# Four transformer layers on one core: the f16 half of the 32-head attentions' probabilities is cast by VectorE instead of computed by a second exponential on ScalarE

## What is computed

```python
q = einsum('bse,ef->bsf', query, Wq)      # 32 heads of 16
k = einsum('bse,ef->bsf', key, Wk)        # 8 heads of 16
v = einsum('bse,ef->bsf', value, Wv)
q, k = q * cos + rotate_half(q) * sin, k * cos + rotate_half(k) * sin   # first layer alone
scores = einsum('bhqd,bhkd->bhqk', q, repeat(k, 4)) / sqrt(16)
out = einsum('bhqk,bhkd->bhqd', softmax(scores), repeat(v, 4))
return einsum('bsf,fe->bse', out, Wo)
```

## Time and profile before

| | |
|---|---|
| median of three runs | 2558.53 us |
| lowest, highest | 2553.02, 2559.68 us |
| the profiled execution | 2555.08 us |
| its span, first to last instruction | 2553.1 us |
| granted TensorE clock, mean share of full speed | 0.918 |
| busy: TensorE, VectorE, ScalarE, GpSimd | 2287.4, 1725.6, 1254.1, 189.3 us |

### The profile page before, as it was taken

How to read it: one execution, slowest core, us unless ns; L and a number is a source line. 1 busy time by engine, 2 the same in 40 slices (tenths; PEclk the granted TensorE clock), 3 DMA queues, 4 the chain that set the end, 5 groups by cost and what they waited for, 6 DMA issues and landing times.

```text
span 2553.1 us, 41949 instructions
## 1 busy us (share of the span) xinstructions
PE 2287.4 (90%) x15456; PEld 1292.8 (51%) x15456; DVE 1725.6 (68%) x4380; ACT 1254.1 (49%) x3499; POOL 189.3 (7%) x191
## 2 busy tenths in 40 slices
PE   4778799989999999999985888799889999999978
PEld 2333344445666666666653444344455555555544
DVE  6443455576777777777767453565778888888873
ACT  3333421136656665666552453433366666666631
POOL 1333300000000000000000133200000000000010
PEclk8666799999999999999998686699989999999999
DMA  4000011110010010010000000001111101110000
GB/s 168 17 9 1 1 50 50 58 59 26 17 42 26 18 42 27 18 42 10 26 17 17 1 34 1 17 17 50 66 42 43 42 18 43 42 42 20 34 1 33
DMA packets 10297, 82.37 MB, mean 32 GB/s; under 512 B 1376, under 2 KB 1376, under 8 KB 2528
## 3 DMA queue, kind: packets, MB, share of 16 engines
q1 hardware_dynamic: 10080, 79.54, 8.6%
HBM read 77.44 MB, written 2.10 MB: 31 GB/s over the span
## 4 chain that ended last, share of the span: by engine, by line
PE 48%; DVE 25%; issue 13%; ACT 10%; POOL 3%; DMA 0%; DVEq 0%; POOLq 0%; ACTq 0%; SPq 0%
PE bank L463 40%; ACT probs L1171 4%; DVE probs L1669 3%; ACT pT_hi L1238 3%; DVE rawmax L1637 3%; DVE qT_lo L1714 2%; DVE pT_lo L1730 2%; POOL pT_lo L419 2%; POOL qT_lo L419 1%; PE bank L810 1%; PE bank L793 1%; DVE oT_lo L1683 1%; PE bank L563 1%; DVE wa_lo L1327 1%; DVE masked L1645 1%
## 5 line engine op out<-in xcount | busy, mean ns | idle before, releaser
L463 PE MATMUL bank<-xnT_hi,wa_hi 128*128 128x512 f16 x736 | 280.6, 381 | 3.2 <-PE bank L463 2.6
L463 PE MATMUL bank<-xnT_lo,wa_hi 128*128 128x512 f16 x736 | 280.1, 381 | 0.0
L463 PE MATMUL bank<-xnT_hi,wa_lo 128*128 128x512 f16 x736 | 280.0, 380 | 0.0
L463 PE MATMUL bank<-wo_hi,oT_hi 128*128 128x512 f16 x576 | 228.0, 396 | 24.7 <-DVE oT_lo L1683 16.2
L463 PE MATMUL bank<-wa_hi,xnT_hi 128*128 128x512 f16 (+3 forms) x672 | 226.8, 343 | 10.0 <-DVE wa_lo L1327 5.2
L1171 ACT ACTIVATE probs<-bank,negmax,rms_r 128x256 f32<-128x256 f32 x256 | 141.0, 560 | 189.2 <-DVE negmax L1642 189.2
L463 PE MATMUL bank<-wo_lo,oT_hi 128*128 128x512 f16 x576 | 228.4, 397 | 0.0
L463 PE MATMUL bank<-wo_hi,oT_lo 128*128 128x512 f16 x576 | 228.3, 396 | 0.0
L463 PE MATMUL bank<-wa_lo,xnT_hi 128*128 128x512 f16 (+3 forms) x672 | 227.1, 343 | 0.0
L463 PE MATMUL bank<-wa_hi,xnT_lo 128*128 128x512 f16 (+3 forms) x672 | 226.7, 343 | 0.0
L1494 DVE TENSOR_REDUCE negmax_n<-bank 128x4 f32<-128x512 f32 x128 | 87.5, 689 | 152.6 <-PE bank L563 152.1
(11 more groups left out here) (256 smaller groups left out, 5555.5 us busy)
## 6 DMA issues: line engine op xcount, KB each, us to landing
raw<-in_w_qkv_dram SPq DMA_DIRECT2D x18, 1536.0 KB, 6.6
raw<-in_w_out_dram SPq DMA_DIRECT2D x18, 1024.0 KB, 4.8
raw<-in_w_ffn_dram SPq DMA_DIRECT2D x15, 1024.0 KB, 4.8
raw<-in_w_ffn0d_dram SPq DMA_DIRECT2D x7, 512.0 KB, 3.4
x<-in_x_dram SPq DMA_DIRECT2D x1, 2048.0 KB, 8.4
expert_b<-in_expert_b_dram SPq DMA_DIRECT2D x1, 2048.0 KB, 9.3
raw<-in_w_ffn3b_dram SPq DMA_DIRECT2D x2, 1024.0 KB, 4.9
out_dram<-x SPq DMA_DIRECT2D x1, 2048.0 KB, 6.3
```

The source lines that it names most:

```text
L463: mm = pe.matmul(dst, l, r, start=start and k == 0, stop=stop and k == n - 1)
```

## The change

ScalarE's second exponential of each unit (L1099) goes, with its wait for `ng_attn`; `ng_exp` is now raised by the first. VectorE gets `probs_hi(j)`: it waits for `ng_exp`, from the fifth unit also for attend(j-4), copies `probs` to the f16 half and raises the new semaphore `ng_phi`, on which GpSimd's `probs_lo(j)` waits in place of `ng_exp`. It stands at the head of step j in VectorE's list. That is so in both stages, 64 units each.

```diff
@@ GpSimd, probs_lo @@
                 J = n * UNITS + j
-                pool.wait_ge(ng_exp, J + 1)
+                pool.wait_ge(ng_phi, J + 1)
@@ ScalarE, soft @@
                     if j >= 4:
                         act.wait_ge(ng_plo, J - 3)
-                        act.wait_ge(ng_attn, J - 3)
                     p32, hi, lo = p_ring(j)
-                    act.activation(p32, bank[PT0 + j % 2][:, :], ACT.Exp)
-                    act.activation(hi, bank[PT0 + j % 2][:, :], ACT.Exp).then_inc(ng_exp, 1)
+                    act.activation(p32, bank[PT0 + j % 2][:, :], ACT.Exp).then_inc(ng_exp, 1)
@@ VectorE, narrow @@
+                def probs_hi(j):
+                    J = n * UNITS + j
+                    dve.wait_ge(ng_exp, J + 1)
+                    if j >= 4:
+                        dve.wait_ge(ng_attn, J - 3)
+                    p32, hi, lo = p_ring(j)
+                    dve.tensor_copy(hi, p32).then_inc(ng_phi, 1)
+
                 q_part(0)
                 kv_part(0)
                 for j in range(-G, UNITS + 5):
                     b, g = divmod(j, G)
                     f, p = b + 1, b + 2
+                    if 0 <= j < UNITS:
+                        probs_hi(j)
                     if g == 0 and f < B:
                         q_rows(f)
```

More of the change, by code:

```diff
@@ L340, in build @@
                              "nb_max_rows", "nb_inv", "nb_on", "nb_olo", "nb_y", "ng_max"))
+        ng_phi = sem("ng_phi")
         n_consts, nb_qn, nb_kn, nb_parts, ng_plo = (sem(n) for n in ("n_consts", "nb_qn", "nb_kn", "nb_parts", "ng_plo"))
```

## The result

| | before | changed |
|---|---|---|
| median of six runs | 2558.5 us | 2572.0 us |
| lowest, highest | 2553.0, 2562.1 | 2565.9, 2579.6 |
| the profiled execution | 2555.08 | 2567.67 |
| its span | 2553.1 | 2565.5 |
| busy ScalarE, VectorE | 1254.1, 1725.6 | 1193.5, 1778.9 |

The ratio is 1.0053, with a 95% interval of 1.0032 to 1.0073: slower by 13.5 us, where 41 were forecast (2596.5, range from 2574). The sign was right and the size was not. The changed kernel's six runs lie in two groups, three at 2566 to 2568 us and three at 2576 to 2580, and its profile is of one of the lower three.

A forecast was written before the change was run, and what follows sets the result against it. TensorE, busy 90%, was taken as the bound, so its waits for VectorE count. 16.4 + 1 + 9.8 - 2.8 + 5 + 12 = 41.4 us on 2555.1 gave 2596.5, range 2574 to 2616.

The forecast's parts named there:

- Prices: 128 exponentials of 0.59 us removed from ScalarE, 128 casts of 0.428 us added on VectorE.
- Step g = 2, +1.17: Both stages, 14 blocks: row maximum 1.45 us later behind the cast, k rows 0.28 earlier; 1.17 each, +16.4 us.
- Steps g = 3 to 5, +1: Maximum again 1.45 us late, but projection matmuls between the two scores cover it; +1 us in all.
- Step g = 6, second stage, +1.4: Seven blocks: cast ahead of max_split adds 0.38 us, its subtraction waiting for GpSimd at the port 1.0; +9.8 in all.
- Step g = 6, first stage, -0.4: Seven blocks: GpSimd's L419 starts earlier, so max_split's subtraction ends at 222.0 instead of 222.39; -2.8 us in all.
- The tails, +5: Units 57 to 63, both stages: the next cast can't run beside L419, 1.68 us per unit; +5 us together.
- The clock, +12: Second stage: more idle at g = 2 and g = 6 lowers the clock, about half of 22.6 us; first stage 0.
- Rival (e): Faster: new idle keeps blocks at clock 0.93, each giving back up to 6.8 us; six give 2543.6; chance 0.06.
- the signs of being right: Listed trace signs of a right forecast, among them second-stage blocks of 30 to 34 us at a clock near 0.66.
- (c): Second stage: VectorE's subtraction gets ahead of GpSimd, 7 us less, and no clock is lost: 2577; chance 0.07.
- (a): Whole kernel: the waits as worked out, but no loss of clock: 2555.1 + 29.4 = 2584.5 us; chance 0.20.
- (d): The late maximum at g = 2 costs nothing, gains and losses within 5 us: about 2557; chance 0.08.

The follow-up runs named there:

- portfree: Changed kernel, with GpSimd's subtraction of the unit at g = 6 held until VectorE's max_split is over: 2560.1 us, ratio 0.9981 to the kernel before.
- tail26: Changed kernel with the casts of g = 2 and g = 6 moved later, and ScalarE's second exponential kept in each stage's last block: 2535.9 us, ratio 0.9905.

## Why the prediction was right or wrong

**Prices**: right. The cast took 0.427 us for 0.428.

**Step g = 2, +1.17**: right as a wait. The row maximum came 1.84 behind its scores (s+1.90 was forecast), the step grew by 1.56 and the one before it shrank by 0.32.

**Steps g = 3 to 5, +1**: right where there are projections: at the full level g = 5 took 2.58 in place of 2.48, the 0.1 that was forecast. But in block b = 6 there is nothing to cover the maxima, and these steps grew by 2.0 in each stage. The prediction had named that price ("each step would cost up to 1.4") and had not seen where it applies.

**Step g = 6, second stage, +1.4**: right. The step g = 6 took 3.45 in place of 2.10, and `portfree` shows the port as the cause of 1.0 of it.

**Step g = 6, first stage, -0.4**: right for six blocks, 4.04 in place of 4.50. The seventh, b = 6, has no rotary products and went from 2.15 to 3.71, as in the second stage. What I had not seen either is that a wait of 1.8 could be taken away at this step.

**The tails, +5**: somewhat too much. In the terms of the earlier trace rows, GpSimd's subtractions alone, seven of them span 1.2 us more in the first stage and 2.6 more in the second:

```profile
281.21:291.59 10.38, 8.07 (x7) 0.69 0.01 2
1634.43:1647.05 12.62, 8.84 (x7) 0.60 0.07 11
```

In the first stage they come every 1.52 us, where 1.68 was forecast. At the turned scores, which run ahead of them, 1.2 and 1.4 had arrived by unit 63. `tail26` gave 3.5 of such time back.

**The clock, +12**: here the prediction failed. It measured about -13 (-16 in the first stage, +2.6 in the second) by the estimate from two blocks and -16 (-18.1 and +1.7) by TensorE's busy time. That is 25 to 28 us below the forecast, and the miss of the whole sum, in the profiled execution, is 41.4 - 12.6 = 28.8. In the second stage the +12 was a loss for every block; the fast blocks did lose (g = 7 of b = 2 at 0.50 in place of 1.00), and the two slow ones won most of it back. I had reasoned that more idle means more time at the lower level, and had put the first stage at 0 with 5 upward, since its clock "already falls at both". That it falls was right. That it also has to rise again, and that this is what an added wait can bring forward, was left out. Before, the clock fell 0.5 us ahead of g = 3, and stayed at 0.50 through g = 3 and 4 and nearly all of g = 5. With the wait it falls 2.0 us ahead of g = 3, so part of the lower stretch lies in idle time, where it costs nothing, and it is back ahead of g = 4. Rival (e) had this mechanism, with 6.8 us a block, but a chance of 0.06 and the wrong reason against it ("More idle hardly does that six times"): four blocks of the first stage did it, in a regular way, and two of the second, each giving back 3 to 4 us and not 6.8. The range took in no gain of clock at all, and so ended at 2574. Part of what came true is luck: the second stage's blocks take 30 to 31 us, as the signs of being right said, but at a clock of 0.78 and not near 0.66, and block b = 6 reaches 30 by waits that were not in the sum.

**The rivals**: (c), 2577, was the nearest in number and falls by its mechanism, since the subtraction does wait for the port. (a), without a loss of clock, 2584.5, is 12 too high. (d) falls with the waits that are there. (e) had the direction of the clock right and its size too large.

What stays open is what decides that the clock rises. In the block before, the level fell at 201.0, just as a busy stretch began. TensorE was busy from 201.0 to 206.9 and from 207.7 to 212.7, each without a break, and the clock stayed down until 218.0. In the changed one the level fell at 193.1, ahead of the busy stretch from 194.7 to 200.4, and was up again at 199.9. The runs show the result for each placing, in most of them regular from block to block, but no rule by which it could have been computed beforehand.

## What to carry to other kernels

A wait moved or added in a loop whose blocks change clock has two prices: its length, and what it does to the stretch at the lower clock. In the first stage the second was twice the first and of the opposite sign (18.1 us back for 8.6 of waiting). So where blocks of the same work differ by 20%, a range has to hold both signs of it, and a trial with a dummy delay in the old kernel shows the sign without writing the change.

A cover found in the usual block is to be looked for in the first and last blocks too. The projections hid the late maxima in six of seven blocks, and the seventh cost 3.6 us in each stage.

In an engine's hand-written list, a new instruction that waits for another engine is best tried behind what others wait for in that step: the same cast, moved behind the row maxima and the split, turned +0.5% into -0.7%, and kept off the last block into -0.95%. One such move is not a gain by itself: behind the maxima alone it left the kernel at +0.7%.

Look for an engine pair that meets at the same event. VectorE's instructions with two SBUF inputs stood still until GpSimd's instruction was over, and a semaphore that releases both at once made them meet in every block of the second stage.

## What the hardware showed

A kernel got faster by 0.35% through added idle time alone: up to 0.6 us in each of 14 blocks took the first stage from 227.7 to 211.1 us in the profiled execution and its granted clock from 0.63 to 0.73. In the second stage 1.3 us added at g = 2 cost 2.1 us over seven blocks, and the same four steps later 8.3.

A VectorE subtraction of 128x32, 0.20 us by itself, took 1.02 to 1.27 when it met a GpSimd instruction of 128x512 that had begun before it, and 0.197 again as soon as the order was turned.
